# Flamingo layer, attention stage: the products of P with the values of all four quads in one group at the end of a unit, with four buffers of P

## What is computed

```
x = x + tanh(g_xattn) * xattn(layernorm(x), ctx, ctx)        # x: 32 batches of 112 tokens of 256; ctx: 32 x 375 x 128
x = x + tanh(g_ffn)   * ffn(layernorm(x))                    # 8 experts of 1024, each takes its 896 best tokens

def xattn(q, k, v):                                          # 16 heads of 16
    qh, kh, vh = heads(q @ Wq + bq), heads(k @ Wk + bk), heads(v @ Wv + bv)
    attn = softmax(einsum('bhqd,bhkd->bhqk', qh, kh) / 4)
    return concat(einsum('bhqk,bhkd->bhqd', attn, vh)) @ Wo + bo
```

## Time and profile before

| | us |
|---|---|
| median of 3 runs | 921.96 |
| the runs | 921.96, 922.36, 918.26 |
| span of the profiled execution, first to last instruction | 920.0 |
| TensorE matmul busy in the span | 842.9 (92%) |
| VectorE busy | 700.1 (76%) |
| ScalarE busy | 576.5 (63%) |

### The profile page before, as it was taken

One profiled execution on the slowest core, in us unless ns is written; L12 is line 12 of the kernel. 1 busy time (PEld: TensorE's weight loads), 2 busy tenths in 40 slices (PEclk: granted clock), 3 DMA queues, 4 the chain that ended last, 5 costly groups with the idle time before them and its releaser, 6 DMA issues. The chain is left out here.

```text
span 920.0 us, 22337 instructions
## 1 busy us (share of the span) xinstructions
PE 842.9 (92%) x8392; PEld 674.8 (73%) x8392; DVE 700.1 (76%) x1900; ACT 576.5 (63%) x1251; POOL 233.9 (25%) x212
## 2 busy tenths in 40 slices
PE   5989999999999999999999404999999999999995
PEld 3545778778777777777777202888888989898885
DVE  6887898898898888888885685787576767674542
ACT  2656776776776776776766112848494756658471
POOL 4750000000000000000000242076465656654404
PEclk9999999999999999999999655999999999999998
DMA  8835675675675576575531301343526253544303
GB/s 189 202 75 116 138 170 141 145 172 134 151 171 145 140 173 146 138 174 146 120 83 33 114 1 29 115 127 91 128 50 138 48 129 57 138 96 105 35 7 41
DMA packets 96212, 104.64 MB, mean 114 GB/s; under 512 B 11745, under 2 KB 92273, under 8 KB 96113
## 3 DMA queue, kind: packets, MB, share of 16 engines
q1 hardware_dynamic: 84128, 88.50, 38.5%
q0 software_dynamic: 10752, 14.69, 9.5%
q10 hardware_dynamic: 1232, 0.12, 0.1%
HBM read 39.60 MB, written 14.68 MB: 59 GB/s over the span
## 5 line engine op out<-in xcount | busy, mean ns | idle before, releaser
L429 DVE TENSOR_REDUCE a_nm<-a_pS 112x1 f32<-112x375 f32 x512 | 265.4, 542 | 50.4 <-PE a_pS L690 46.9
L287 ACT ACTIVATE a_P<-a_pT 128x448 f32<-128x448 f32 x258 | 139.3, 548 | 61.7 <-PE a_pT L684 60.4
L690 PE MATMUL a_pS<-a_kst,a_qst 96*112 96x375 bf16 x512 | 154.4, 331 | 3.3 <-DVE a_nm L429 2.4
L1640 PE MATMUL e_p<-w2hl,e_hh 128*128 128x512 f32 x440 | 156.9, 397 | 0.0
L684 PEld LDWEIGHTS a_pT<-a_qst,a_kst 98*128 98x128 bf16 x1536 | 110.5, 99 | 41.0 <-issue 10.9
L684 PE MATMUL a_pT<-a_qst,a_kst 98*128 98x112 bf16 x1536 | 133.7, 213 | 2.2 <-ACT a_P L287 1.3
L1642 PE MATMUL e_p<-w2hl,e_hl 128*128 128x256 f32 x440 | 122.9, 279 | 0.0
L1434 POOL DMA_INDIRECT out_dram<-e_y,e_idx x56 | 89.3, 1595 | 110.6 <-ACT e_y L1473 104.6
L1146 POOL MEMSET r_factors<- 128x1 f32 x12 | 0.5, 103 | 458.0 <-POOLq L62 457.8
L1520 DVE TENSOR_TENSOR e_hl<-e_hid,e_hh 128x384 fp32r<-128x384 f32 (+1 forms) x128 | 77.9, 624 | 47.2 <-ACT e_hh L1466 46.3
L1640 PEld LDWEIGHTS e_p<-w2hl,e_hh 128*128 128x128 f32 x440 | 82.5, 187 | 18.6
(11 more groups left out here) (237 smaller groups left out, 1554.2 us busy)
## 6 DMA issues: line engine op xcount, KB each, us to landing
a_kst<-a_kp SPq DMA_DIRECT2D x192, 192.0 KB, 3.5
w<-in_L_ffn_W_dram SPq DMA_DIRECT2D x16, 1024.0 KB, 7.1
a_qst<-a_qp SPq DMA_DIRECT2D x96, 112.0 KB, 3.6
a_craw<-in_ctx_dram SPq DMA_DIRECT2D x32, 128.0 KB
a_room<-in_x_dram SPq DMA_DIRECT2D x8, 448.0 KB, 6.2
a_xb<-in_x_dram SPq DMA_DIRECT2D x32, 112.0 KB, 2.9
out_dram<-a_x SPq DMA_DIRECT2D x32, 112.0 KB, 1.9
xn_scratch<-a_x SPq DMA_DIRECT2D x32, 112.0 KB, 2.1
```

Of the source, the lines that this page charges most:

```text
L287: act.activation(P[(4 * b + quad) % 3][:, c, :], pT[u % 2][:, 0:4 * LQ], ACT.Exp).then_inc(exp_done, 1)
L429: dve.tensor_reduce(nm[:, h:h + 1], pS[h % 2][0:LQ, 0:LK], AXX, ALU.max, negate=True).then_inc(s_used, 1)
L690: pe.matmul(pS[h % 2][0:LQ, 0:LK], q_of(b, slice(0, ROWS), h), kst[b % 4][0:ROWS, h, 0:LK], start=True, stop=True).then_inc(s_ready, 1)
L1640: pe.matmul(p2[g % 2][:], hh[:, f, rows], T.w2hl[r % 2][:, f].rearrange("p q d -> p (q d)"), start=(f == 0), stop=(f == 7), skip_group_che ...
```

## The change

W0 moves from step 7 to step 11, ahead of W1, W2 and W3, so that the 48 matmuls of a batch stand in one group. As the exponentials of the next quads then come before the P of quad 0 is read, a fourth buffer of P is made, in a further part of `room` (which is free by then), and quad q always has `P[q]`. The values, the banks, the waits and the sums stay as they were.

```
-        P.append(room[:, 0:12 * LQ].rearrange("p (c n) -> p c n", c=3))
+        P += [room[:, i * 12 * LQ:(i + 1) * 12 * LQ].rearrange("p (c n) -> p c n", c=3) for i in range(2)]
...
-                act.activation(P[(4 * b + quad) % 3][:, c, :], pT[u % 2][:, 0:4 * LQ], ACT.Exp).then_inc(exp_done, 1)
+                act.activation(P[quad][:, c, :], pT[u % 2][:, 0:4 * LQ], ACT.Exp).then_inc(exp_done, 1)
...
-                                         P[(4 * b + quad) % 3][0:n, c, j * LQ:(j + 1) * LQ], start=(c == 0), stop=(c == 2),
+                                         P[quad][0:n, c, j * LQ:(j + 1) * LQ], start=(c == 0), stop=(c == 2),
...
-                    if u == 7 and live(m + 1):
-                        weighted(m + 1, 0)
                     if u == 7 and live(m - 1):
                         bank_free(m, A_PIECES, 7)
                         pe.wait_ge(x2_ready, m)
...
                     if u == 11 and live(m + 1):
-                        for quad in range(1, 4):
+                        for quad in range(4):
                             weighted(m + 1, quad)
```

## The result

The changed kernel took 932.41 us (median of 4 runs, 931.67 to 932.57) against 920.11 us before (4 runs on the same chip, 917.55 to 922.36). The ratio is 1.013, with a 95% interval of 1.011 to 1.015: slower by 1.3%, about 12 us. The profiled execution, of 932.5 us, has a span of 930.8 us, 10.8 more than before.

The account below looks back on a forecast made before the run. TensorE bounds the kernel, closely coupled with VectorE. 28 units x 0.345 us = 9.7, less 0.4 for the first two units, plus 0.7 for the last two, gives +10.0 on 921.96: 932.0 us, eight-in-ten range 925 to 938.

Parts of the forecast that it names:

- The price of W0 in the group: Group at the unit's end: a fourth quad adds 0.595 us, making the group last about 2.47 us.
- The saving of the edges: Tiling-mode changes around W0 in step 7: moving it saves TensorE 0.215 us of its own work a unit.
- The stall at X: Step 7: TensorE waits for x2, 0.47 us after S2 is through; X starts 0.28 us sooner, at least 0.19.
- the sum: Per unit: 0.595 us for the longer group less 0.25 gained at X, 0.345 us longer; 28 units, 9.7 us.
- The limit by the transposes of the context: Behind X: these wait for ScalarE's copy of the maxima, so at most 0.25 us of the gain survives.
- X starts about 0.55 us after S2: Sign in the changed profile, every unit: X released by line 490 after some 0.5 us of TensorE idle.
- The delay goes through VectorE, back to TensorE at the keys, and on to X.: From S10 to the next X: the whole 0.345 us delay is passed on, unit about 14.10 us.
- The 9% rival: Key product: TensorE's 0.17 us wait swallows part of the delay, 0.175 us a unit lost, 927.2 us; 9%.
- X's other condition ... is not what is late.: Step 7: ScalarE's copy of cc ends at 398.91, before x2 at 399.11, so it does not delay X.
- The ends: Four units outside the 28: first two -0.4 us together, last two +0.7 (bounds -0.4 to +1.2).
- They gain the edges: First two units, with W0 but no X: each gets 0.215 us shorter, -0.4 us together.
- The rival of the drain alone: Whole attention loop: edges saved and nothing waits, 32 units x 0.215 = 6.9 us faster, 915.1 us; 10%.

Follow-up runs that it names:

- e2: Changed kernel with W0 left out altogether, so the products of quad 0 are not computed; 914.6 us, 13.53 us a unit.
- e10: e9 with W0 back in step 7 behind S2 and three quads in the group at the end; 919.7 us, 13.73 us a unit.
- e9: Changed kernel with X, both other transposes and T4 moved, last layernorm link before S1's maximum, x2's copy before ScalarE's key part; 924.5 us.
- e8: Changed kernel with T4 moved ahead of the key product for which TensorE waits; 931.5 us, 14.11 us a unit.
- e11: Changed kernel with the maximum of head 15 taken over 16 keys instead of 375, shortening VectorE's row; 932.8 us, 14.10 us a unit.
- e12: Changed kernel with both the short maximum of head 15 and T4 ahead of the key product; 929.4 us, 14.00 us a unit.
- e3: Changed kernel with the last layernorm link ahead of the maximum of S1 on VectorE, so x2 comes earlier; 932.3 us, 14.10 us a unit.
- e1: Kernel before with only the fourth buffer of P added, W0 staying in step 7; 921.4 us, 13.76 us a unit.

## Why the prediction was right

The prediction was right in its number and, for the unit, in its mechanism: 932.0 us forecast, 932.4 measured, 14.10 and 14.11 us for a unit. That the totals agree to 0.4 us is in part luck. The forecast added 10.0 us to 921.96, the median of three runs; against 920.11, the median of the four, the change measured 12.3 us, and between the two spans 10.8. By its own steps:

- **The price of W0 in the group**, 0.595 us, the group 2.47: measured 2.45, and 0.58 in the unit by e2.
- **The saving of the edges**, 0.215 us, is seen in rows and in the time of no run. In step 7 W0 adds 0.78 us between S2 and T8 (1.01 in e10, 0.23 in e9), in the group 0.57: 0.21 for the edges. In the changed kernel the stall hides it in every unit.
- **The stall at X.** x2 came 0.47 us after S2 was through, as worked out. The hand-over took 0.145 us, not 0.06; that is the value which the end of the stage had shown. So X comes 0.20 us sooner than before. By the group the gain is 0.23 us, where the sum had 0.25, and the group itself takes 0.58 us more, where the sum had 0.595. The limit by the transposes of the context did not bind. Two small errors cancel, which is luck too. The sign "X starts about 0.55 us after S2" counts from where S2 is through; there 0.61 us were measured, 0.77 from its start.
- **"The delay goes through VectorE, back to TensorE at the keys, and on to X."** The size was right, the route was only one of two. e8 shows that VectorE's row alone carries the delay of S10 to x2; e11 that the way over the keys and TensorE does too; only both together (e12) free it. The 9% rival, which had TensorE's wait at the keys swallow part, is out: that wait is 10.3 us in 26 units, against 10.2 before.
- **"X's other condition ... is not what is late."** True of X, but I did not look one and two places further. e3 shows that the copy of the values and the copy of x2 stand behind x2 at nearly the same time. The forecast did not need it; advice drawn from it (bring x2 forward) would have been wrong.
- **The ends.** This step failed: "They gain the edges" is wrong for both first units. In the first, which has no X, it is 7.05 us from S2 to the copy of O before (82.76 to 89.81) and 7.40 after (82.18 to 89.58), a loss of 0.35 us where -0.215 was forecast. W0 had covered a wait for the copy of the values, which stands in the changed kernel as

```profile
83.25 0.22 PE L733 MATMUL a_pM<-identb,a_mm 112*32 112x112 bf16 x1 [0.39 <-ACT a_V L314]
```

  The second (m = 0) lost 0.50 (13.92 against 13.42 us), with 0.59 us of the same wait. The last four distances of O's copies grew by 0.27, 0.40, 0.41 and 0.69 us; the last of them is not steady (9.69 us before, 8.53 in e1, whose order is the same). The four units that the forecast prices apart thus cost about 1.95 us, not 0.3. The whole account: the profiled run of the changed kernel reached the first unit 0.58 us sooner, which is not the change's doing; then +0.35 + 0.50 + 9.4 + 1.77 make the last copy of O 11.4 us later, and about 0.65 us are given back behind it. The 9.4 are 26 units, one with 0.32 us extra. The error at the ends, about 1.7 us, hardly shows in the total.
- **The rival of the drain alone** (faster, 915.1 us) fails, by the stall.

What stays open: whether some order saves the edges and opens no wait, and what a group of four would then be worth. Neither e9 nor any other run has such an order.

## What to carry to other kernels

When a piece of work is moved, ask what was finishing on other engines while it ran, and not only for the first instruction behind it: several waits may be stacked under the same cover (here for x2, the values and the copy of x2), and curing the first shows the second. A reordering that takes one wait away can make another: with the link ahead of a maximum (e9), the score product that needed this maximum waited. An engine that stands idle behind a long group has cost nothing as long as the distance between the products that follow stays the same; measure that distance before blaming the group. Do not compare absolute times of two profiles either, but distances from an instruction ahead of the change. When the units repeat exactly, a chain closed from one instruction to the same one in the next unit, through each engine, gives the time of the unit almost to the hundredth; where two engines tie, no single edit shows either.

## What the runs showed of the hardware that was not expected

- The time from VectorE's last link to X on an idle TensorE was 0.145 us in all 28 units, while from its key part (line 453) to the key product it was 0.06 before, and from ScalarE's copies to waiting TensorE also 0.05 to 0.07 (e3). The trace shows a likely reason, which no run tried. TensorE's wait for x2 is an instruction of its own on its queue: it starts 0.04 us after the link ends and takes 0.05, the weight load follows 0.025 us later and X 0.03 after that. The waits for the keys and for the copies in e3 are carried by the weight load itself, which starts 0.05 us after the end of what it waits for.
- A unit of the changed kernel took 14.43 us instead of 14.11: in it the second half of the group took longer, without a wait for another engine:

```profile
228.00 1.66 PE L701 MATMUL a_pO<-a_room,a_V 128*32 128x112 f32 x48
```

  against 1.34 us in the others. Of the 0.32 us, 0.22 show as one idle time of the weight loads inside the group, with no releaser. Its cause was not tried.
